# Edge-row phase of a four-layer graph network: messages, tile sums, their copies and scatters put in another order

## The reference, cut to what matters

```python
x = _layernorm(x + _L1(x, ...))            # scale, shift, max(a, 0.01 a), + 2 x1, layer norm
hs = xs @ w_in2f_s / sqrt(B)               # 128 scalar columns -> 32
hv = einsum('nbc,bf->nfc', xv, w_in2f_v)   # 3 x 128 vector columns -> 3 x 32
s, v = hs[idx_j], hv[idx_j]                # idx_j is dst
t_s1, t_s2, t_v1, t_v2 = s*y0, <v,yv>, s*yv, v*y0   # each times a filter of the edge
agg = segment_sum(edge, idx_i)             # idx_i is src
```

## Time and profile before

| | us |
|---|---|
| median of 3 runs | 2283.05 (2282.64 to 2285.45) |
| the profiled execution | 2283.68 |
| its span, first to last instruction | 2282.0 |
| busy over the span: PE, DVE, ACT, POOL | 1894.0, 1505.0, 1161.8, 938.4 |
| mean granted PE clock | 0.892 |
| edge phase, 1513 to 1704: busy PE, DVE, ACT, POOL | 81.0, 120.3, 99.2, 89.2 of 191 |
| granted PE clock in the edge phase | 0.50 |

### The profile page before, as it was taken

The page is one execution under the profiler, slowest core; times in us unless marked ns, Lnnn a source line. Parts: engine busy times, 40 slices in busy tenths (PEclk is TensorE's granted clock), DMA queues, the critical chain, the costliest instruction groups (busy, mean ns, idle before and its releaser), DMA issues. The chain is left out here.

```text
span 2282.0 us, 25087 instructions
## 1 busy us (share of the span) xinstructions
PE 1894.0 (83%) x5922; PEld 970.1 (43%) x5922; DVE 1505.0 (66%) x2634; ACT 1161.8 (51%) x2333; POOL 938.4 (41%) x1048
## 2 busy tenths in 40 slices
PE   5999998599999999999999948624435999999930
PEld 2444443244444444444444425313323555555510
DVE  5365553277777777777777648177637877777867
ACT  2344443255555555555555412245537777777744
POOL 3212112266666666666666655445531111111026
PEclk9999999799999999999999968855556999999975
DMA  7742112444444444444444365533327443443444
GB/s 256 243 167 62 19 14 37 143 146 150 159 158 156 154 154 150 150 150 150 154 158 156 126 226 110 90 105 79 81 50 269 167 151 133 155 151 128 147 148 148
DMA packets 146225, 316.65 MB, mean 139 GB/s; under 512 B 18817, under 2 KB 32034, under 8 KB 145638
## 3 DMA queue, kind: packets, MB, share of 16 engines
q1 hardware_dynamic: 114646, 235.45, 29.4%
q0 software_dynamic: 28160, 75.82, 13.2%
q10 hardware_dynamic: 3344, 4.51, 0.7%
HBM read 176.64 MB, written 139.79 MB: 139 GB/s over the span
## 5 line engine op out<-in xcount | busy, mean ns | idle before, releaser
L667 PE MATMUL d_p_h<-w3a,d_xT 128*128 128x512 f32 x632 | 287.1, 597 | 25.1 <-DMA d_xT<-in_xT 25.1
L667 PE MATMUL d_p_o<-d_w,d_uT 128*128 128x512 f32 x632 | 286.2, 596 | 3.0 <-ACT d_uT L742 3.0
L667 PE MATMUL d_p_p<-d_wr,d_x1T 128*128 128x512 f32 x632 | 288.4, 600 | 0.0
L552 POOL TENSOR_SCALAR d_small<-d_mv 128x1 f32<-128x1 f32 x158 | 80.8, 512 | 299.6 <-DVE d_mv L793 151.6
L824 DVE TENSOR_TENSOR d_zz<-d_yg,d_xbeta 128x512 f32<-128x512 f32 x79 | 136.9, 1733 | 97.7 <-POOL d_yg L875 97.7
L667 PEld LDWEIGHTS d_p_h<-w3a,d_xT 128*128 128x128 f32 x632 | 121.1, 192 | 178.5 <-issue 178.5
L667 PEld LDWEIGHTS d_p_o<-d_w,d_uT 128*128 128x128 f32 x632 | 120.3, 191 | 154.9 <-issue 150.3
L735 ACT ACTIVATE d_yn<-d_y,d_small 128x512 f32<-128x512 f32 x79 | 64.3, 813 | 228.5 <-POOL d_small L557 228.5
L667 PEld LDWEIGHTS d_p_p<-d_wr,d_x1T 128*128 128x128 f32 x632 | 115.6, 193 | 116.6 <-issue 116.6
L763 ACT ACTIVATE d_x<-d_zz,d_small 128x512 f32<-128x512 f32 x79 | 64.2, 813 | 175.3 <-POOL d_small L557 175.3
L284 PE MATMUL m_p_H<-m_xT,m_w 128*128 128x512 f32 x320 | 147.3, 615 | 4.8 <-ACT m_xT L325 4.8
(11 more groups left out here) (275 smaller groups left out, 4345.1 us busy)
## 6 DMA issues: line engine op xcount, KB each, us to landing
state<-d_empty SPq DMA_DIRECT2D x80, 264.0 KB, 2.1
sum<-m_tile_sum SPq DMA_DIRECT2D x10, 2048.0 KB
pair_rows<-p_rows SPq DMA_DIRECT2D x40, 512.0 KB
pair_x<-x SPq DMA_DIRECT2D x40, 512.0 KB
out_rows<-pair_rows SPq DMA_DIRECT2D x40, 512.0 KB
d_xT<-in_xT SPq DMA_DIRECT2D x79, 256.0 KB
d_z<-sum SPq DMA_DIRECT2D x79, 256.0 KB
d_x<-in_x SPq DMA_DIRECT2D x79, 256.0 KB
```

The source lines that it names most:

```text
L552: nc.gpsimd.tensor_scalar(tmp, var, factor, add, ALU.mult, ALU.add).then_inc(done, 1)
L667: last = nc.tensor.matmul(out[:, :], lhsT[:, c, :], w[:, c, :], start=(c == 0), stop=(c == KB - 1))
```

## The change

Only the order of steps on each engine changes. DVE makes the message of a tile two tiles behind norm, not one. PE does the tile sum of u-2 ahead of turn(u) and features(u), where it did that of u-1 behind them. ACT copies the sum of three tiles back, between x2_rows and turn_out. POOL scatters tile t-4 ahead of the gathers, where it scattered t-2 behind them. The loops are longer by the added depth. Instructions, buffers and waits stay.

```diff
--- before.py
+++ after.py
@@ -1318,12 +1318,12 @@
             for u in (1, 0, 3, 2):
                 gather(u)
             set_eps(nc, k, pool)
-            for t in range(T + 2):
+            for t in range(T + 4):
+                if 0 <= t - 4 < T:
+                    scatter(t - 4)
                 if t + 2 < T:
                     gather(2 * t + 5)
                     gather(2 * t + 4)
-                if 0 <= t - 2 < T:
-                    scatter(t - 2)
             pool.wait_ge(scattered, 16 * T)
 
         @block.vector
@@ -1380,11 +1380,11 @@
                 nc.vector.tensor_reduce(e4[:, 0, 1, :], part[b][:, :].rearrange("p (c f) -> p f c", c=3), AX_X,
                                         ALU.add).then_inc(edge_done, 1)
 
-            for t in range(T + 1):
+            for t in range(T + 2):
                 if t < T:
                     norm(t)
-                if t:
-                    message(t - 1)
+                if t >= 2:
+                    message(t - 2)
 
         @block.scalar
         def _(act):
@@ -1416,12 +1416,13 @@
 
             nc.scalar.preload_act_table_set(ACT_SET)
             act.wait_ge(k.eps_set, 2)
-            for t in range(T + 1):
+            for t in range(T + 3):
                 if t < T:
                     x2_rows(t)
+                if t >= 3:
+                    sum_out(t - 3)
+                if t < T:
                     turn_out(t)
-                if t:
-                    sum_out(t - 1)
 
         @block.tensor
         def _(pe):
@@ -1455,12 +1456,12 @@
                                  ).then_inc(s_done, 1)
 
             pe.wait_ge(w_in, 32)
-            for u in range(T + 1):
+            for u in range(T + 2):
+                if u >= 2:
+                    tile_sums(u - 2)
                 if u < T:
                     turn(u)
                     features(u)
-                if u:
-                    tile_sums(u - 1)
 
 
 def equivariant_phase(nc, k):
```

## The result

The changed kernel takes 2244.33 us (median of 4 runs, 2242.94 to 2244.83) beside 2283.57 for the kernel before. The ratio is 0.9826, with a 95% interval of 0.9809 to 0.9843: 39.2 us less. The profiled execution took 2244.56 us, with a span of 2242.9.

A forecast was written before the change was run, and what follows sets the result against it. The prediction took a ring of waits between ACT and PE, 8.53 us a tile, as the bound, with DVE's 6.16 next. 40.0 us won less 1.4 in the drain, net 38.6, gave 2244.4 us, range 2239 to 2257.

The forecast's parts named there:

- The ring of ACT and PE: Edge phase: sum copy, squares, transposes, their copy, features and sum matmul each await the last, 8.53 us a tile.
- DVE at 6.16 us a tile: DVE's own work sets the new pace: norm 5.25, step to message 0.08, message 0.83 us.
- r(2) to r(19): Starts of L1360 in tiles 2 and 19, taken as 17 tiles of 6.16 us apart.
- ACT's and PE's cover: ACT needs some 5.3 us of each 6.16; PE's added wait before the transposes is hidden with 1.2 us.
- POOL: Scatter, p gather and x gather, held by DVE instructions, take about 1.9, 1.3 and 1.6 us; with gaps 5.7 a tile.
- below 6.16, though by little: POOL's 5.7 us a tile leaves only 0.4 us below DVE's pace.
- rival B: POOL becomes the bound through holds, 6.6 to 7.1 us a tile, kernel 2252 to 2261 us; chance 0.08.
- rival C: POOL is held over several DVE instructions, gathers land late: 10.8 us a tile, kernel slower, 2324 us; chance 0.03.
- POOL's order needed: POOL's scatter(t-4) ahead of two gathers makes them wait for a sum copy; p gather's landing hidden with 1.8 us to spare.
- The drain: After the last L1360, four scatters 4.48 us apart; the last starts 18.5 us later, giving back 1.4 us.
- The sum: Edge phase: 40.0 us won up to the last L1360, 1.4 given back, net 38.6 us; median 2244.4.

The follow-up runs named there:

- x1_dve_only: Kernel before with only DVE's part of the change (message two tiles behind norm): 0.9998 of the kernel before, steady tile 8.53 us.
- x2_dve_back: Changed kernel with DVE's message set back to one tile behind norm: 0.9893 of the kernel before, tiles 6.32 and 7.21 us in turn.
- x8_pe_back: Changed kernel with PE's order undone, the tile sum of u-2 behind turn and features: 0.9831 of the kernel before, steady tile 6.21 us.
- x3_pool_back: Changed kernel with POOL's old loop, gathers first and then scatter(t-2): 0.9949 of the kernel before, tile 7.8 us on average.
- x4_sum2: Changed kernel with ACT's sum copy two tiles behind, not three, and the scatter three, not four: 0.9820 of the kernel before.
- x9: The changed kernel itself, run again for comparison: 0.9827 of the kernel before, steady tile 6.21 us.
- x10: Changed kernel with a POOL memset of 128x1024 added in tiles 4 to 17: 0.9895 of the kernel before, steady tile 7.37 us.
- x5_no_leaky: Changed kernel without L1347, the leaky relu of the edge rows on DVE: 0.9756 of the kernel before, steady tile 5.3 us.
- x6: Changed kernel with sum copy two and scatter three tiles behind, and negated mean (L1360) moved from DVE to ACT: 0.9789 of the kernel before.
- x11: Changed kernel with the added POOL memset of 128x1024 and the negated mean moved from DVE to ACT: 0.9807 of the kernel before, tile 5.97 us.

## Why the prediction was right, point by point

- **The ring of ACT and PE as the bound**: shown by x1_dve_only, which leaves the ring and gains nothing, and by x2_dve_back, which opens it and gains two thirds. That it is the place of ACT's sum copy that opens it is argued from the earlier trace rows and from x8_pe_back, where PE's order is undone without loss; no run sets ACT's order back alone.
- **DVE at 6.16 us a tile**: 6.15 to 6.18 in 15 of the 17 steady tiles, 6.54 and 6.52 in two. From r(2) to r(19) it is 105.6 us, where 17 x 6.16 = 104.7 was summed. Some 0.7 of the 0.9 us are the two long tiles, 4 and 12, whose message begins 0.45 and 0.43 us behind L1360 and not 0.08; the prediction had no such term, and its cause stays open. That POOL makes L1360 longer (the prediction had only looked at DVE holding POOL) isn't the reason: twelve tiles have the longer L1360 without the delay, and x3_pool_back has the delay in tile 12 without it:

```profile
1588.07 0.17 DVE L1360 TENSOR_SCALAR e_neg<-e_total 128x2 f32<-128x2 f32 x1
...
1588.50 0.29 DVE L1371 TENSOR_TENSOR e_edge<-e_p_F,filters 128x128 f32<-128x128 f32 x1 [0.26 <-PE e_p_F L1445]
```

The bracket names the features that PE had made last, but those are tile 11's; the message here is tile 10's, and its features were done at 1579.85. Tiles 4 and 12 are late in the same way in x3, x4, x8, x9 and x10, and none is where DVE's loop is one instruction shorter (x5, x6, x11). x5_no_leaky shows that DVE and nothing else made the pace.
- **ACT's and PE's cover**: ACT waits in 18 tiles for DVE, PE's transposes for the rows. x8_pe_back shows that PE's order is free, x4_sum2 that one tile less of distance would have been enough for the sum.
- **POOL**: the scatter, p and x gather take 1.98, 1.31 and 1.59 in ten of the tiles (the first three rows of the tile shown above), for 1.9, 1.3 and 1.6 in the prediction; laying each on the DVE instruction beside it worked. The conclusion drawn from it, "below 6.16, though by little", and with it rival B's price, failed. x5_no_leaky ran POOL at 5.3 us a tile and x11 gave it 1.6 us more at 5.97. The holds are no fixed work: when POOL is late, its operations start elsewhere and are held less. In all twelve traces, a gather that began more than 0.15 us before the end of one of norm's instructions (L1338 to L1356, all with two SBUF inputs, of which L1347 reads one tile twice) ended 0.81 to 0.87 us behind that end (320 gathers), and a scatter 1.45 to 1.51 (176); the others took 0.94 to 1.00 and 1.55 to 1.63. So the hold is what is left of the instruction in which the operation begins. The hold of more than one instruction, on which rival C rested, was met nowhere: in no run did a scatter take over 2.61 us, with 1.55 its shortest: 1.06 of hold, less than one L1345 of 1.23.
- **POOL's order needed**: the prediction said what it queues (gathers behind a sum copy) and found it hidden; it said nothing of what the old order would have cost. x3_pool_back shows 24.7 us.
- **The drain**: 18.6 us, for 18.5 summed; four scatters 4.52 to 4.58 apart, for 4.48. x4_sum2 shows that their number is what counts: one less, 4.5 us less.
- **The sum**: 38.6 us in the phase were predicted and 37.6 measured; that the median fell on the predicted 2244.4 to a tenth owes 1.5 us to stretches outside the phase, which differ from one execution to the next.

The Trainium skill (SBUF — State Buffer, Who interferes with whom) says that the ports shared by DVE and GpSimd are locked, for the whole instruction, by the one that starts first, and counts `tensor_scalar` among the DVE instructions that can ask for them. x10 and x11 agree that a tensor_scalar can be held so: 1.84 us for 0.17, beside a memset of 1.58. Which one started first they don't show, since L1364's record begins 0.22 us before the memset's. The same section has a DVE instruction with two SBUF inputs contend only with GpSimd instructions that read SBUF, and takes the making of descriptors for a write. Here an indirect gather took 1.88 us when issued inside the two-input L1345, and 0.95 alone; that it reads its list of indices from SBUF would fit, but no run separates that.

## What to carry to other kernels

Where no engine is full, write down the ring as a list of starts from one turn of the timeline, and ask of each engine which instruction stands ahead of the one that could go on; then check that the reordering opens every ring, since here one engine's order alone brought nothing and another's, left as it was, took back two thirds. The last full engine's own work gives the new pace to 1%; the tiles still open at the end give the drain. When an engine gets full, look at its smallest instructions beside the others': moving one of 0.17 us away won 0.20 us in an ordinary tile, 0.24 on average, and made the phase robust against more POOL work.

## What the runs showed of the hardware

- A DVE tensor_scalar of 128x2 took 0.30 us in place of 0.17 beside an indirect scatter, without delaying the message behind it, and 1.84 beside a memset of 128x1024 on POOL (x10). Beside the same memset, once it was gone (x11), a tensor_tensor with PSUM and SBUF inputs, a tensor_reduce and a tensor_tensor with two SBUF inputs kept their 0.25, 0.27 and 0.68 us.
- An indirect gather took 0.95 us alone and up to 1.88 when issued inside a DVE instruction with two SBUF inputs; a scatter 1.55 and up to 2.61 (in x2_dve_back). The longest hold, 1.06, is less than the 1.23 us of DVE's longest instruction. A held gather ended 0.81 to 0.87 us and a held scatter 1.45 to 1.51 us behind the end of the DVE instruction in which it began, in all twelve traces.
- Scatters in the drain, each waiting for the one before, follow one another 4.42 to 4.60 us apart (the ends of this range are from x3 and x10).
